# Where the causal mask of an attention row-max pass is added: two TensorE products, or an add inside VectorE's maximum

## What is computed

```python
q = (x @ Wq).reshape(B, S, 32, 16).transpose(0, 2, 1, 3)   # 32 heads of 16
k = (x @ Wk).reshape(B, S, 8, 16).transpose(0, 2, 1, 3)    # 8 key/value heads, 4 query heads each
q, k = rope(q), rope(k)
scores = jnp.einsum('bhqd,bhkd->bhqk', q, k) / jnp.sqrt(16)
scores = jnp.where(causal, scores, -max_float)
probs = jax.nn.softmax(scores, axis=-1)
out = jnp.einsum('bhqk,bhkd->bhqd', probs, v) @ Wo
```

## Time and profile before

| | us |
|---|---|
| median of 3 runs | 2278.55 |
| lowest, highest | 2272.32, 2315.87 |
| the profiled execution | 2303.76 |
| its span, first to last instruction | 2301.7 |

### The profile page before, as it was taken

One profiled execution on the slowest core, in us unless ns is written; L12 is line 12 of the kernel. 1 busy time (PEld: TensorE's weight loads), 2 busy tenths in 40 slices (PEclk: granted clock), 3 DMA queues, 4 the chain that ended last, 5 costly groups with the idle time before them and its releaser, 6 DMA issues.

```text
span 2301.7 us, 41702 instructions
## 1 busy us (share of the span) xinstructions
PE 1964.9 (85%) x12707; PEld 976.5 (42%) x12707; DVE 1314.6 (57%) x2831; ACT 1042.5 (45%) x1568; POOL 718.4 (31%) x985
## 2 busy tenths in 40 slices
PE   6999979989999799889997979899979688998930
PEld 3434335544333355543343545334345344444410
DVE  4588836546798265468982654688736312222248
ACT  2557753334677433446774334567733222222200
POOL 2212214522222145222222452122215422222248
PEclk9889989987899899979998999799989899999975
DMA  2122323310000121100001110000002199999988
GB/s 84 55 93 94 127 87 111 137 54 2 11 16 12 33 98 67 38 6 11 12 12 42 62 59 21 6 12 12 16 28 75 62 300 322 335 335 315 339 252 293
DMA packets 108130, 232.81 MB, mean 101 GB/s; under 512 B 24423, under 2 KB 24423, under 8 KB 107920
## 3 DMA queue, kind: packets, MB, share of 16 engines
q1 hardware_dynamic: 81072, 191.07, 23.9%
q0 software_dynamic: 24576, 35.07, 6.3%
q10 hardware_dynamic: 2272, 4.06, 0.5%
HBM read 141.59 MB, written 126.48 MB: 116 GB/s over the span
## 4 chain that ended last, share of the span: by engine, by line
PE 59%; DVE 12%; issue 10%; DMA 7%; ACT 3%; POOL 2%; DVEq 2%; SPq 1%; another core or an unknown queue 1%; POOLq 1%; ACTq 0%
PE ps L759 9%; DVE rmax L1212 8%; PE ps L698 7%; PE ps L653 6%; DMA gx<-dispatch_scratch 6%; PE ps L898 5%; PE ps L845 4%; PE ps L779 4%; PE ps L871 3%; PE ps L930 3%; PE ps L884 3%; PE ps L654 3%; PE ps L673 2%; PE ps L872 2%; PE ps L705 2%
## 5 line engine op out<-in xcount | busy, mean ns | idle before, releaser
L1212 DVE TENSOR_REDUCE rmax<-ps 128x1 f32<-128x512 f32 (+3 forms) x1280 | 732.5, 632 | 188.0 <-PE ps L708 114.2
L1038 ACT ACTIVATE pr<-ps 128x1024 f32<-128x1024 f32 (+3 forms) x768 | 586.2, 813 | 239.4 <-PE ps L779 233.2
L698 PE MATMUL ps<-kT,qT 48*128 48x512 f16 (+3 forms) x1536 | 396.5, 349 | 34.0 <-DVE rmax L1212 23.8
L759 PE MATMUL ps<-pr,v_ones 128*32 128x512 f32 (+3 forms) x3072 | 348.1, 528 | 7.9 <-POOL pr L1488 4.5
L1488 POOL TENSOR_SCALAR_AFFINE_SELECT pr<-pr 128x512 f32<-128x512 f32 x256 | 162.2, 638 | 502.5 <-ACT pr L1038 501.1
L779 PE MATMUL ps<-qT,kT 50*128 50x512 f16 (+3 forms) x1536 | 301.4, 344 | 17.0 <-ACT pr L1038 7.9
L698 PEld LDWEIGHTS ps<-kT,qT 48*128 48x128 f16 x1536 | 123.3, 95 | 343.8 <-DVE rmax L1212 282.8
L1534 POOL DMA_INDIRECT dispatch_scratch<-x,slot_i x192 | 190.1, 990 | 73.4 <-issue 73.4
L705 PE MATMUL ps<-above,sel 64*128 64x128 bf16 x1024 | 190.1, 227 | 0.0
L898 PE MATMUL ps<-gu_sb,gxT 128*128 128x384 f32 x512 | 189.0, 493 | 0.0
L1553 POOL DMA_INDIRECT acc_scratch<-eo,etok x64 | 98.7, 1541 | 282.5 <-DVE eo L1351 270.3
(11 more groups left out here) (149 smaller groups left out, 2599.0 us busy)
## 6 DMA issues: line engine op xcount, KB each, us to landing
gu_sb<-w_gu_dram SPq DMA_DIRECT2D x64, 768.0 KB, 7.6
dn_sb<-w_dn_dram SPq DMA_DIRECT2D x64, 384.0 KB, 9.0
dispatch_scratch<-blank SPq DMA_DIRECT2D x8, 2308.0 KB, 8.8
gx<-dispatch_scratch SPq DMA_DIRECT2D x64, 288.5 KB, 5.2
xin<-x_dram SPq DMA_DIRECT2D x32, 256.0 KB
acc_scratch<-blank SPq DMA_DIRECT2D x32, 256.0 KB, 2.1
xres<-x_dram SPq DMA_DIRECT2D x32, 256.0 KB
x_scratch<-x SPq DMA_DIRECT2D x32, 256.0 KB, 2.0
```

The source lines that it names most:

```text
L698: last = pe.matmul(o, qT[r:r + SROWS, half, 2 * g + h // 2, q % QPH * P:(q % QPH + 1) * P], kT[r:r + SROWS, g, kh * HALF:kh * HALF + w], s ...
L759: last = pe.matmul(ps[32 * h:32 * h + 32, 6, c0:HALF], v_ones[g % 2][:, kt, :], pr[i % SLOTS][:, h, 0:HALF - c0], start=kt == 0, stop=kt = ...
L1038: act.activation(pr[i % SLOTS][:, 2 * pair:2 * pair + 2, 0:HALF - c0], ps[:, 2 + 2 * pair:4 + 2 * pair, 0:HALF - c0], ACT.Exp, scale=facto ...
L1212: dve.tensor_reduce(dst[:, heads[0] % 2, heads[0] // 2:heads[0] // 2 + n, q % QPH], ps[:, BANK_OF[item], 0:n * w].rearrange("p (h k) -> p ...
```

## The change

On PE the two mask products of each diagonal head go, and with them `sel`, `above` and the eight instructions of POOL that make them. A constant `future` of 128 x 512 float32 comes, zero but for its last 128 columns, which hold the large negative number above the diagonal; its last w columns are the mask of a unit of width w. On DVE a diagonal unit is no longer one `tensor_reduce`: each head has a `tensor_tensor_reduce`, which reads the scores in PSUM and the mask in SBUF, writes their sum back over the scores in PSUM, and gives the maximum of the sum to `rmax`. So there are 1024 of these and 512 of the old reductions (were 1280). The wait of a diagonal unit becomes a `wait_apart`, and the wait on `max_ready` moves ahead of it. The planner's two costs change with it: DVE is priced 0.065 more for the second head of a diagonal unit, PE no longer has the 0.086. So the three planned orders may come out another way.

```diff
--- before.py
+++ after.py
@@ -176,7 +176,7 @@
             if redq and redq[0] in scored:
                 item = redq.pop(0)
                 w, heads = UNITS[item[2]][3:]
-                now["dve"] = red[item] = max(now["dve"], scored[item] + LAT) + 0.065 + len(heads) * w / 960
+                now["dve"] = red[item] = max(now["dve"], scored[item] + LAT) + 0.065 + len(heads) * w / 960 + (0.065 * (len(heads) - 1) if UNITS[item[2]][1] // QPH == UNITS[item[2]][2] else 0)
                 if item[2] == NU - 1:
                     now["dve"] = red[item] = now["dve"] + 0.3
                 continue
@@ -281,7 +281,7 @@
                 moved[items[0]] = now["pe"] + DRAIN
             else:
                 half, q, kh, w, heads = UNITS[items[0][2]]
-                now["pe"] = at + len(heads) * (w / 2400 + 0.004 + (0.086 if q // QPH == kh else 0))
+                now["pe"] = at + len(heads) * (w / 2400 + 0.004)
             for item in items:
                 scored[item] = now["pe"] + DRAIN
                 held[BANK_OF[item]] = item
@@ -322,8 +322,7 @@
         shdn_sb = sb("shdn_sb", [P, SIC, D], f32, att)
         ropec_sb = sb("ropec_sb", [P, TT, HD], f32, att)
         ropes_sb = sb("ropes_sb", [P, TT, HD], f32, att)
-        sel = sb("sel", [P, 2, P], bf16, att)
-        above = sb("above", [P, P + ROWT], bf16, att)
+        future = sb("future", [P, HALF], f32, att)
         wmax = sb("wmax", [P, 2], f32, att)
         wtop = sb("wtop", [2, 1], f32, att)
         wdiag = sb("wdiag", [2, 2], f32, att)
@@ -686,29 +685,14 @@
 
                 def score_units(items):
 
-                    g = items[0][1]
-                    for k in range(len(UNITS[items[0][2]][4])):
-                        stage = []
-                        for item in items:
-                            half, q, kh, w, heads = UNITS[item[2]]
-                            h = heads[k]
+                    for item in items:
+                        half, q, kh, w, heads = UNITS[item[2]]
+                        for k, h in enumerate(heads):
                             r = ROWT * (h % 2)
-                            o = ps[:, BANK_OF[item], k * w:(k + 1) * w]
-                            diag = q // QPH == kh
-                            last = pe.matmul(o, qT[r:r + SROWS, half, 2 * g + h // 2, q % QPH * P:(q % QPH + 1) * P],
-                                             kT[r:r + SROWS, g, kh * HALF:kh * HALF + w], start=True, stop=not diag)
-                            if diag:
-                                stage.append((o, r, w))
-                            elif k == len(heads) - 1:
-                                last.then_inc(sc_done, 1)
-                        for o, r, w in stage:
-                            pe.matmul(o[:, w - P:w], sel[r:r + ROWT, 0, :], above[r:r + ROWT, r:r + P],
-                                      start=False, stop=False)
-                        for o, r, w in stage:
-                            last = pe.matmul(o[:, w - ROWT:w], sel[r:r + ROWT, 1, :], above[r:r + ROWT, r:r + ROWT],
-                                             start=False, stop=True)
-                            if k == len(heads) - 1:
-                                last.then_inc(sc_done, 1)
+                            last = pe.matmul(ps[:, BANK_OF[item], k * w:(k + 1) * w],
+                                             qT[r:r + SROWS, half, 2 * item[1] + h // 2, q % QPH * P:(q % QPH + 1) * P],
+                                             kT[r:r + SROWS, item[1], kh * HALF:kh * HALF + w], start=True, stop=True)
+                        last.then_inc(sc_done, 1)
 
                 def max_transpose(item, bank):
                     half = int(item[0] == "t1")
@@ -1203,15 +1187,25 @@
                 def reduce_unit(item):
 
                     half, q, kh, w, heads = UNITS[item[2]]
-                    dve.wait_ge(sc_done, PER_BATCH * b + RANK[item] + 1)
                     n = len(heads)
                     if item[1] and item[2] in (0, NU0):
                         dve.wait_ge(max_ready, 2 * (KVH * b + item[1]) - 1 + (item[2] == NU0))
+                    if q // QPH == kh:
+                        wait_apart(dve, sc_done, PER_BATCH * b + RANK[item] + 1)
+                    else:
+                        dve.wait_ge(sc_done, PER_BATCH * b + RANK[item] + 1)
                     base = 16 * (half + kh)
                     dst = rmax[:, base:base + 16].rearrange("p (r h q) -> p r h q", r=2, q=QPH)
-                    dve.tensor_reduce(dst[:, heads[0] % 2, heads[0] // 2:heads[0] // 2 + n, q % QPH],
-                                      ps[:, BANK_OF[item], 0:n * w].rearrange("p (h k) -> p h k", k=w),
-                                      AX, ALU.max).then_inc(sc_reduced, 1)
+                    if q // QPH == kh:
+                        for k, h in enumerate(heads):
+                            score = ps[:, BANK_OF[item], k * w:(k + 1) * w]
+                            last = dve.tensor_tensor_reduce(score, score, future[:, HALF - w:HALF], 1.0, NEG, ALU.add, ALU.max,
+                                                            dst[:, h % 2, h // 2:h // 2 + 1, q % QPH])
+                        last.then_inc(sc_reduced, 1)
+                    else:
+                        dve.tensor_reduce(dst[:, heads[0] % 2, heads[0] // 2:heads[0] // 2 + n, q % QPH],
+                                          ps[:, BANK_OF[item], 0:n * w].rearrange("p (h k) -> p h k", k=w),
+                                          AX, ALU.max).then_inc(sc_reduced, 1)
                     if item[2] == NU - 1:
                         dve.drain()
                         dve.tensor_tensor(rmax[:, 16:32], rmax[:, 16:32], rmax[:, 32:48], ALU.max).then_inc(parts_joined, 1)
@@ -1405,8 +1399,7 @@
             for m in (id_h, id_f):
                 pool.memset(m[:], 0.0)
             pool.memset(minus_half[:], -0.5)
-            pool.memset(sel[:], 0.0)
-            pool.memset(above[:], 0.0)
+            pool.memset(future[:], 0.0)
             pool.memset(before[:], 0.0)
             pool.memset(ones_b[:], 1.0)
             for k in range(2):
@@ -1419,14 +1412,8 @@
                 pool.affine_select(out=m[:], in_=m[:], compare_op=ALU.not_equal, fill=1.0, base=0,
                                    pattern=[[-1, P]], channel_multiplier=1)
 
-            for k in range(2):
-                part = sel[:, k, ROWT * k:ROWT * k + ROWT]
-                for base in (0, -ROWT):
-                    pool.affine_select(out=part, in_=part, compare_op=ALU.not_equal, fill=1.0, base=base,
-                                       pattern=[[-1, ROWT]], channel_multiplier=1)
-                    pool.drain()
-            pool.affine_select(out=above[:], in_=above[:], compare_op=ALU.is_ge, fill=NEG, base=0,
-                               pattern=[[-1, P + ROWT]], channel_multiplier=1)
+            pool.affine_select(out=future[:, HALF - P:HALF], in_=future[:, HALF - P:HALF], compare_op=ALU.is_ge, fill=NEG, base=0,
+                               pattern=[[-1, P]], channel_multiplier=1)
 
             pool.affine_select(out=before[:], in_=before[:], compare_op=ALU.is_ge, fill=1.0, base=0,
                                pattern=[[-1, P]], channel_multiplier=1)
```

## The result

The changed kernel takes 2401.59 us (median of 4 runs, 2385.21 to 2433.82); the kernel before, run beside it, 2297.21 (4 runs, 2272.32 to 2326.33). The ratio is 1.051 with an interval of 1.038 to 1.065: slower. (Executions of one kernel differ by 2 to 3% among themselves, so each ratio is taken from the faster runs of both kernels, and is not that of the medians.) The forecast was 2330, in a range of 2240 to 2440. The direction and the range held; the loss of 104 us is twice the 51 worked out, and most of it comes from another place.

What follows compares the result with a forecast made beforehand. Bound: TensorE and VectorE both nearly full in 25.8 us steady periods, VectorE the slower afterwards. Per batch 13.8 + 0.5 - 1.5 = 12.8 us, four batches +51: 2278.55 + 51 = 2330 us, range 2240 to 2440.

Steps and rivals of the forecast that it cites:

- What bounds the kernel: Steady periods between row-max joins, 25.8 us each: TensorE busy for 24.86 and VectorE for 22.93, both nearly full.
- TensorE's 2.9 us: Per steady period, 32 diagonal heads lose both mask products, 0.09 us each: TensorE's 24.86 us becomes 22.0.
- The columns: VectorE's diagonal units: 1.04 ns a column as before; reading the mask and writing the sum to PSUM add 0.
- The second output: VectorE's new instruction also gives the maximum, through an accumulator read: 0.11 us a head, 3.5 us per period.
- rival 1: On VectorE, the second output is free: period 24.6 us, total 2241 us; decides under 0.04 us a head; chance 0.20.
- Planner prices: The planner prices VectorE's new work too low; this moves waiting around, no cost of its own while VectorE is slower.
- The clock at 1.00: In the steady periods, TensorE was to stay at full clock, busy for 22 us or less of 28.1.
- Rival 3: In steady periods, TensorE's idle pieces bring its clock down: period 34 us, +8.2, total 2472 us; chance 0.10.
- The sum: Steady period: VectorE 27.1 us plus 1.0 of gaps makes 28.1 against 25.8, +2.3; four batches +51 us.
- Free output: The same as rival 1: VectorE's maximum is written by the same instruction at no extra cost; 2241 us, chance 0.20.
- Dear output: On VectorE, the second output costs 0.28 us as on ACT: period 33.2 us, total 2475 us; chance 0.18.
- turns in PSUM: VectorE reads and writes one bank in turns: 10.7 us more per period, some 2600 us; within Dear output's 0.18.

Runs made afterwards that it cites:

- The order alone: The kernel before with the change's two planner prices, so only the three planned orders differ, no instruction changed: 1.047 of before (1.034 to 1.061).
- the run with the measured prices: The changed kernel with its planner given 0.115 us per diagonal head on VectorE and 3.6 us to the row in qT: 1.052 of before (1.040 to 1.064).

## Why the prediction was right in direction and half in size

- **What bounds the kernel: right, and not carried far enough.** Two nearly full engines, TensorE the longer. TensorE stood idle for 0.9 of 25.8 us in a steady period of before, no piece over 0.24 us, and the clock held; the prediction used this only as a budget.
- **TensorE's 2.9 us: half of it is there, worth 0.9.** Without the products TensorE's busy time in a full-clock period goes from 24.9 to 23.5, not to 22.0, and the period from 25.8 to 24.9, where VectorE is busy for 22.8. With the whole change TensorE is busy for 24.2 at full clock and for 25.3 to 30.6 in after's periods, where 22 or less was to be the sign.
- **The columns: right.** (720 - 588) / 128 = 1.03 ns a column with two operands and the sum written back to PSUM, against 1.04. Writing the bank that is read costs nothing per column. The separate wait was taken at 0; the equal steps of 0.25 us with and without it bear that out where VectorE doesn't idle.
- **The second output: the instruction was seen right, its price was three times too high.** There are the forecast 1024 accumulator reads, 140 ns each. But the next instruction starts with the read: the step is 0.65 for 0.614, 0.036 us a head where 0.11 was taken. With it VectorE comes to 22.93 + 0.64 + 32 x 0.036 = 24.7; measured are 25.1, forecast were 27.1. That is almost exactly rival 1's break-even of 0.038. The period at full clock is 26.8 all the same and not 25.8, because the engine's gaps grew: 26.8 - 24.9 = 1.9, where 1.0 was kept.
- **Planner prices "not a cost of its own": wrong.** The order alone costs 1.047, mostly through a transfer that was late by 1.4 us and had been covered by a longer list, which nobody had planned for. The working had looked at the bank slots only, not at what the shorter list lets arrive too early.
- **The clock at 1.00: the step that failed.** Rival 3 had it at 0.10: "beyond that it decides". Measured are 0.74 to 0.94 in the period rows of batch 0. The bound set there, that pieces under 1 us matter little, doesn't hold: the run with the measured prices has no stall over 0.5 us in its steady periods and none of them at 1.00. How long one piece must be stays open; stalls of 0.66 us stand beside falls in most periods and without one in 763.59:790.36. The prediction had a section of the Trainium skill for it ("TensorE: Matmul & The Clock Gate", "A second HAM failure mode: psum-queue depth-cycling") and set it aside, because in before the banks cycle at 1.00. But in before TensorE hardly idles between them. Where the idle moments come that the section speaks of, the traces agree with it: with VectorE's new work alone 5 of 28 periods held the clock where before has 22.
- **The sum.** 24 steady periods were to grow by 2.3 us each, 55 in all. They grew from a mean of 26.0 to 30.2, by 100. About 24 of it (24 x 1.0) is the change's work at full clock; the other 76 is, by subtraction, the clock and the waits beside its falls; the 1.0 rests on one period. The second joins took 1.7 us a batch instead of 0.5, and the rest of the batch gave back 5.4 us where 1.5 was taken. That the forecast came as near as it did, and 2401.59 inside the range, owes something to luck: two errors of opposite sign, VectorE's work priced too high and the clock at nothing.
- **Rivals.** Free output: its price was nearly right, its result wrong, since it too kept the clock at 1.00. Dear output and turns in PSUM: excluded by the steps. Clock: what decides here, its size (34 us a period) too large for the measured 30.2.

## What to carry to other kernels

When TensorE is the engine that is busy nearly all the time, taking work from it and giving it to the engine that frees its banks can cost twice: once for the work, and again because TensorE now waits and its clock falls. Before pricing an exchange, ask which engine will wait afterwards. A planner's list hides wrong latencies as long as it is full; after any change of prices, look for a new wait that ends on a transfer. And if two stalls can cause the same symptom, remove them together before you acquit one.

## What the runs showed of the hardware beyond that

- An accumulator read of 140 ns on VectorE runs beside the next instruction; its visible price was 0.036 us, with a separate wait ahead of the instruction included.
- With VectorE's new work and nothing else changed, full-clock periods went from 22 to 5 and, without the mask products, from 10 to 1. Falls stood beside stalls of 0.67 us, but also without any of 0.4 us; one period with a stall of 0.66 us kept its clock. Stretches at half clock lasted from 3 to 20 us.
- The kernel with mask products and the new instruction, given 2.4 us more of busy TensorE per period, had 18 full-clock periods for 5, and was not shown to be faster: its 28 periods took 854.3 us for 842.1.
- The same expert stage of the same kernel took 353.9 us in one execution and 406.6 in another, with the clock at 1.00 and 0.94.
